# Attention in a four-layer transformer stack: values as the stationary operand with a block of ones for the sums, and a new order at the opening and at the seam

## What is computed

```python
for l in range(4):
    h = rmsnorm(x, n1[l])
    q, k, v = split(h @ Wqkv[l].T + bqkv[l])                 # 16 heads of 8
    o = merge_heads(softmax(rope(q) @ rope(k).T * 8 ** -0.5 + causal) @ v)
    x = x + o @ Wo[l].T + bo[l]
    h2 = rmsnorm(x, n2[l])
    kc, vc = split(memory @ Wkv_c[l].T)
    x = x + merge_heads(softmax((h2 @ Wq_c[l].T) @ kc.T * 8 ** -0.5 + cross_bias) @ vc) @ Wo_c[l].T
    h3 = rmsnorm(x, n3[l])
    x = x + silu(h3 @ Wg[l].T) * (h3 @ Wu[l].T) @ Wd[l].T
```

## Time and profile before

| | |
|---|---|
| median of 3 runs | 500.36 us (498.70 to 501.63) |
| the profiled execution: own time, span | 499.64 us, 497.5 us |
| PE busy, PEld busy | 465.2 us (94%), 401.7 us (81%) |
| DVE, ACT, POOL busy | 358.0 us (72%), 268.5 us (54%), 227.9 us (46%) |
| opening until the first projection (L608) | 0 to 16.8 us |
| four layers | to 214.9 us |
| seam until the next block runs steadily | 214.9 to some 226 us |
| later blocks | to 497.5 us |

### The profile page before, as it was taken

How to read it: one execution, slowest core, us unless ns; L and a number is a source line. 1 busy time by engine, 2 the same in 40 slices (tenths; PEclk the granted TensorE clock), 3 DMA queues, 4 the chain that set the end, 5 groups by cost and what they waited for, 6 DMA issues and landing times. The chain is left out here.

```text
span 497.5 us, 14297 instructions
## 1 busy us (share of the span) xinstructions
PE 465.2 (94%) x5430; PEld 401.7 (81%) x5430; DVE 358.0 (72%) x1025; ACT 268.5 (54%) x718; POOL 227.9 (46%) x342
## 2 busy tenths in 40 slices
PE   3899999999999999968999998899999998999997
PEld 3667887788778876967999887789999887689997
DVE  4395668566856786656887889999989987654643
ACT  4377757775777577614334475556466554442221
POOL 2871377137613851243799322767889322300000
PEclk9999999999999999979999999999999999999999
DMA  8601020101029000040210432031020000000000
GB/s 252 276 3 32 10 84 2 40 22 65 3 64 381 2 3 1 2 130 17 70 49 24 157 111 67 2 133 60 10 69 3 2 1 1 1 2 1 12 1 12
DMA packets 9953, 27.08 MB, mean 54 GB/s; under 512 B 1346, under 2 KB 4759, under 8 KB 9623
## 3 DMA queue, kind: packets, MB, share of 16 engines
q1 hardware_dynamic: 9878, 26.09, 15.5%
HBM read 25.82 MB, written 0.26 MB: 52 GB/s over the span
## 5 line engine op out<-in xcount | busy, mean ns | idle before, releaser
L913 POOL TENSOR_TENSOR rstd<-ss,par 128x1 f32<-128x1 f32 x52 | 28.5, 549 | 100.8 <-ACT sq L737 100.8
L759 ACT ACTIVATE pr<-sd 128x512 f32<-128x512 f32 x56 | 34.5, 626 | 5.4 <-DVE sd L816 4.9
L1243 POOL TENSOR_TENSOR xh<-xh,rsx 128x512 f32<-128x512 f32 (+1 forms) x32 | 29.8, 931 | 2.5
L1241 POOL TENSOR_TENSOR xh<-cx,mvx 128x512 f32<-128x512 f32 (+1 forms) x32 | 29.4, 918 | 2.7 <-DMA cx<-ctx_in 1.4
L741 ACT ACTIVATE h<-y,rstd 128x128 f32<-128x128 f32 x48 | 19.1, 399 | 9.5 <-POOL rstd L913 9.4
L1222 DVE BATCH_NORM_STATS2 stx<-cx 128x6 f32<-128x128 f32 x104 | 22.7, 276 | 0.5 <-DMA cx<-ctx_in 0.5
L1772 POOL TENSOR_TENSOR rstd<-mv,par 128x1 f32<-128x1 f32 x20 | 4.1, 207 | 39.8 <-DVE mv L1602 36.3
L737 ACT ACTIVATE sq<-y 128x129 f32<-128x129 f32 x52 | 15.9, 306 | 10.0 <-DVE y L847 8.6
L907 POOL TENSOR_TENSOR kblk<-qk,cf 128x512 f32<-128x512 f32 x20 | 20.8, 1040 | 0.9
L1232 POOL TENSOR_TENSOR rsx<-rsx,par 128x13 f32<-128x13 f32 x8 | 20.4, 2546 | 0.6
L1791 POOL TENSOR_SCALAR rk<-kss 128x8 f32<-128x8 f32 (+1 forms) x32 | 7.5, 235 | 24.0 <-DVE kss L1668 22.5
(11 more groups left out here) (570 smaller groups left out, 1507.2 us busy)
## 6 DMA issues: line engine op xcount, KB each, us to landing
cx<-ctx_in SPq DMA_DIRECT2D x13, 768.0 KB
we<-we_in SPq DMA_DIRECT2D x8, 514.0 KB, 7.1
wc<-wc_in SPq DMA_DIRECT2D x4, 768.5 KB, 5.8
wa<-wa_in SPq DMA_DIRECT2D x5, 387.0 KB, 3.0
wb<-wb_in SPq DMA_DIRECT2D x4, 256.5 KB, 3.8
uvT<-uvT_in SPq DMA_DIRECT2D x1, 1024.0 KB, 7.1
uv<-uv_in SPq DMA_DIRECT2D x1, 1024.0 KB, 8.6
cx<-ctx_in SPq DMA_DIRECT2D x13, 32.5 KB
```

The source lines that it names most:

```text
L759: nc.scalar.activation(pr[:, t, at:at + 512], sd[:, t, at:at + 512], ACT.Exp).then_inc(s[piece], 1)
L913: nc.gpsimd.tensor_tensor(rstd[:, t:t + 1], ss[:, t:t + 1], par[:, 1:2], ALU.pow).then_inc(s[piece], 1)
L1241: step(pool, "pool_step", nc.gpsimd.tensor_tensor(part, cx[u % 2][:, tiles, :], mvx[:, b, tiles, 0].unsqueeze(2).to_broadcast(shape), ALU. ...
L1243: nc.gpsimd.tensor_tensor(part, part, rsx[:, b, tiles].unsqueeze(2).to_broadcast(shape), ALU.mult).then_inc(xm["c_normed"], 1)
```

## The change

1. In `weigha`, `weighb` and `cweigh` the operands change places. The values, spread with zeros to 32 columns (vblk and vcblk), are the stationary operand, and 64 tokens of the turned weights are moving. Four products with 32 columns each write the four groups of 32 rows of one bank. Four more products per half (`ones8` stationary, 128 tokens moving) write the sums next to them, each repeated in 8 rows. A half is 8 + 4 products instead of 8.
2. The result comes out turned. turn_o, oT, cturn_o and coT are gone; `recip` and `crecip` now take 128 x 128 instead of 128 x 16, and `o` and `co` write oT. The bias of the values moves into vblk, whose two copies become two additions (L806 before).
3. `out` reads the rows of Wo in another order (`heads`), made on the host.
4. The opening: x is the first transfer, seg_in comes as one row first and spread later; `mem4` is copied by DVE instead of ACT; vblk and vcblk are cleared by one POOL memset, and by no other piece; memory, mem_k, kc and mem_v of layer 0 go in between the pieces of its self-attention (`FIRST`).
5. The seam: on PE `fast` is now the Else, so that PE jumps over `whole` at the start. ACT's four square_f and what DVE does after z_norm of tile 1 stand behind the If. All tables have new numbers, and so the queues a new order.

```diff
             elif piece in ("weigha", "weighb"):
-                for j in range(4 * (half == "b"), 4 * (half == "b") + 4):
-                    for b in range(2):
-                        last = nc.tensor.matmul(bank[L * b:L * b + L, 18 * j:18 * j + 18], pts[:, t, P * j + L * b:P * j + L * b + L],
-                                                vblk[:, t, b, j, :, :], start=True, stop=True)
+                for b in range(2):
+                    for k in range(4):
+                        j = 4 * half + k
+                        at = 32 * j - 16 * half
+                        nc.tensor.matmul(bank[32 * k:32 * k + 32, L * b:L * b + L], vblk[:, t, b, at:at + 32],
+                                         pts[:, t, P * j + L * b:P * j + L * b + L], start=not half and b == 0, stop=True, skip_group_check=True)
+                for k in range(4):
+                    j = 4 * half + k
+                    last = nc.tensor.matmul(bank[32 * k:32 * k + 32, P:2 * P], ones8[:, 16 - 16 * half:48 - 16 * half], pts[:, t, P * j:P * j + P],
+                                            start=False, stop=True, skip_group_check=True)
                 last.then_inc(s[piece], 1)
-            elif piece in ("turn_o", "cturn_o"):
+            elif piece == "cturn_o":
...
-                pe.wait_ge(s["oT"], n)
+                pe.wait_ge(s["o"], n)
...
-            elif piece == "oT":
-                act.wait_ge(s["turn_o"], n)
-                nc.scalar.activation(oT[:, t, :], held(od, "turn_o", l, t)[:, 0:P], ACT.Identity,
-                                     bias=A[:, A_BV:A_BV + 1]).then_inc(s["oT"], 1)
...
-                nc.vector.reciprocal(rv[:, t, :], ops[:, :, 8]).then_inc(s[piece], 1)
+                nc.vector.reciprocal(qk[:, t, 0, :], held(od, k, l, t)[:, P:2 * P]).then_inc(s[piece], 1)
...
-                nc.vector.tensor_tensor(o[:, t, :].rearrange("p (h d) -> p h d", d=HD), ops[:, :, 0:8],
-                                        rv[:, t, :].unsqueeze(2).to_broadcast([P, H, HD]), ALU.mult).then_inc(s[piece], 1)
+                nc.vector.tensor_tensor(oT[:, t, :], held(od, k, l, t)[:, 0:P], qk[:, t, 0, :], ALU.mult).then_inc(s[piece], 1)
...
         def sp_opening(sp):
-            sp.dma_start(segr[:], seg_in.to_broadcast([P, B * L])).then_inc(s["seg_loaded"], 16)
             sp.dma_start(x[:], x_in.rearrange("(t p) d -> p t d", p=P)).then_inc(s["x_loaded"], 16)
+            sp.dma_start(segi[:], seg_in).then_inc(s["row_loaded"], 16)
+            sp.dma_start(cf[:], cf_in).then_inc(s["cf_loaded"], 16)
+            load_a(sp, 0)
             sp.dma_start(memT[:], memT_in).then_inc(s["mem_loaded"], 16)
             load_b(sp, 0)
...
-                either(pe, lambda: opening(pe, x_pe_piece, pe_piece, "PE"), whole)
+                either(pe, lambda: opening(pe, x_pe_piece, pe_piece, "PE"), whole, falls="end")
```

More of the change, by code:

```diff
@@ L55 @@
 CG = [range(c, min(c + 4, CT)) for c in range(0, CT, 4)]
-PERIOD, SKEW = 95.43, (0.0, 6.74, 13.36, 19.85)
+PERIOD, SKEW = 95.50, (0.0, 6.67, 13.27, 19.91)
 AT = {
[L62 to L74, removed]
@@ new lines @@
+    "PE": {"memory": -54.70, "turn1": -6.09, "project": 0.00, "values": 3.82, "causal": 13.16, "scores": 13.61,
+           "turna": 21.31, "turnb": 21.52, "weigha": 22.05, "weighb": 25.05, "out": 30.41, "turn2": 36.31, "qc": 38.94,
+           "cmask": 41.20, "cscores": 41.43, "cturn": 49.89, "cweigh": 53.17, "cturn_o": -343.21, "cout": 56.79,
+           "turn3": 63.35, "gate": 68.43, "up": 70.12, "down": 81.04},
+    "ACT": {"square1": -15.22, "norm1": -9.46, "mem_k": -47.81, "hT1": -6.71, "q_groups": 8.81, "expa": 15.57,
+            "expb": 18.42, "turneda": 19.96, "turnedb": 21.09, "square2": 29.73, "norm2": 33.72, "hT2": 34.50,
+            "qcT": 36.40, "cexp": 45.30, "cturned": 47.91, "coT": -343.21, "square3": 58.24, "norm3": 59.91,
+            "hT3": 64.58, "tanh": 66.74},
@@ L79 @@
 HOLDS = {
-    1: {"memory": ("mem_k", "mem_v"), "turn1": ("hT1",), "turna": ("turneda",), "turnb": ("turnedb",), "weigha": ("o",), "turn_o": ("oT",), "out": ("y1",), "turn2": ("hT2",),
+    1: {"memory": ("mem_k", "mem_v"), "turn1": ("hT1",), "turna": ("turneda",), "turnb": ("turnedb",), "weigha": ("o",), "out": ("y1",), "turn2": ("hT2",),
         "qc": ("qcT",), "cturn": ("cturned",), "cweigh": ("co",), "cturn_o": ("coT",), "cout": ("y2",), "turn3": ("hT3",),
@@ L86 @@
 BEHIND = "cturn_o cout turn3 gate up down coT square3 hT3 tanh y2 norm3 gated hidden y3 pow3".split()
-SELF = ("turn1 project values causal scores turna turnb weigha weighb turn_o out hT1 q_groups expa expb turneda turnedb oT rope vblk "
+SELF = ("turn1 project values causal scores turna turnb weigha weighb out hT1 q_groups expa expb turneda turnedb rope vblk "
         "maxa maxb shifta shiftb recip o y1 "
@@ L122 @@
 LAYER = {e: list(pieces) for e, pieces in AT.items()}
-FINAL = {"PE": {}, "ACT": {"square_f": 0.18}, "DVE": {"norm_f": 4.73, "x_f": 6.55, "z_moments": 10.88, "z_norm": 17.41},
-         "POOL": {"pow_f": -7.85, "z_power": 0.96}}
+FINAL = {"PE": {}, "ACT": {"square_f": 44411.67}, "DVE": {"norm_f": 37724.60, "x_f": 37726.01, "z_moments": 37727.40, "z_norm": 37735.68},
+         "POOL": {"pow_f": 35574.92, "z_power": 41054.99}}
 for e in AT:
     PLACE.update({p: PLACE["y3"] - PERIOD + a for p, a in FINAL[e].items()})
-FAST = Order({e: [(p, range(LAYERS)) for p in LAYER[e]] + [(p, [LAYERS]) for p in FINAL[e]] for e in AT}, late)
+TURNED = ("cturn_o", "coT")
+FAST = Order({e: [(p, range(LAYERS)) for p in LAYER[e] if p not in TURNED] + [(p, [LAYERS]) for p in FINAL[e]] for e in AT}, late)
 GENERAL = Order({e: [(p, range(LAYERS)) for p in LAYER[e] if p not in CROSS] + [(p, [LAYERS]) for p in FINAL[e]]
@@ L245, in __init__ @@
                       for e in AT}
-        self.first = {e: 1 + max(n for n, z in enumerate(q) if z[1] == 0) for e, q in self.queue.items()}
+        self.first = {e: 1 + max(n for n, z in enumerate(q) if z[1] == 0 and not (e == "ACT" and z[2] == LAYERS) and
+                                 not (e == "DVE" and z[2] == LAYERS and z[3:] != (1, "z_norm"))) for e, q in self.queue.items()}
+        self.rest = {z[2:] for e, q in self.queue.items() for z in q[self.first[e]:] if z[1] == 0}
         FAST.bank, LAST.bank = {}, {}
```

231 lines of the change are left out of this document (127 added, 104 removed).

## The result

The changed kernel takes 502.64 us (median of 20 runs), the kernel before 499.25 us (20 runs): a ratio of 1.0062, with an interval of 1.0045 to 1.0080. It is 0.6% slower where no change was forecast. The profiled execution took 501.80 us against 499.64, its span 500.0 against 497.5, so that the traces hold 2.5 of the roughly 3 us.

The account below looks back on a forecast made before the run. The prediction took PE's queue to bound the kernel in the layers. Its terms, −2.3 − 0.7 − 3.1 + 1.1 + 2.0 + 1.2 + 1.4 + 0.5, summed to +0.1, so 499.7 us, with a range of 493 to 508.

Parts of the forecast that it names:

- Reciprocal: On DVE in the layers: 1.0 us for 128x128, 0.74 more each, delaying PE by +1.4 us in four layers.
- weigh: On PE: 56 halves at 0.50 us instead of 0.48, +1.1 us in all.
- The turns: On PE: 36 turns of o removed at 0.11 us each, less 0.9 for waits that grow, −3.1 us.
- the new wait: In the layers: weigha waits for ACT's copy behind adjacent turna and turnb of tile 0, once per layer, +1.2 us.
- modes: On PE in the four layers: 12 more changes of array part size at 0.17 us each, +2.0 us.
- The opening: Start of the kernel: first scores 3.0 us earlier despite PE's jump, one memory of 0.67 still to do, −2.3 us.
- The later blocks: In the last attention: longer chains from weighb through recip to out, +0.5 us.
- Rival B: In the layers: DVE makes PE wait, maxima standing behind long reciprocals; 506.3 or 507.7 us, chance 0.16.
- A: Layers and start: charged waits and mode changes fall into PE's free time, start gives −3.5; 493.4 us, chance 0.32.
- C: On PE: pitch of starts doesn't fall, 0.72 us a half instead of 0.48; 512.0 us, chance 0.09.
- D: On PE: only two column groups work at once, 1.0 us a half; 527.7 us, chance 0.03.
- seam: Between layers and later blocks: down starts some 0.7 us earlier, z_turn some 2.9 us after y3 of tile 3; −0.7 us.

Follow-up runs that it names:

- experiments 3: Changed kernel with the layer numbers of before (PERIOD, SKEW, AT), without turn_o and oT, two opening numbers later; 1.0243 of the kernel before.
- 5: Changed kernel with the numbers of before in layers 1 to 3 on all engines; 0.9972 of the kernel before.
- experiment 15: Changed kernel with PE's numbers of before in layers 1 to 3 and PE's jump back at the seam, run again; 0.9981 of the kernel before, median 499.39 us.
- Experiment 8: Changed kernel with PE's If as before, so that PE jumps at the seam; 1.0044 of the kernel before.
- experiment 2: Kernel before with the reciprocal working on 128 columns, nothing else moved; 1.0300 of the kernel before.
- 7: Kernel before without turn_o, oT, cturn_o and coT; 0.9882 of the kernel before.
- 10: Changed kernel with PE's numbers of before in layers 1 to 3 and PE's jump back at the seam; 0.9940 of the kernel before.
- 11: Changed kernel with all engines' numbers of before in layers 1 to 3 and PE's jump back at the seam; 0.9954 of the kernel before.
- 13: Kernel before without turn_o, oT, cturn_o and coT and with the reciprocal over 128 columns; 0.9922 of the kernel before.
- experiment 1: Changed kernel with its reciprocals working on 16 of the 128 columns; 1.0013 of the kernel before.

## Why the forecast was wrong

**The terms of the change itself were near.** Reciprocal: 1.0 us forecast, 0.95 measured; DVE 39.7 a layer forecast, 39.05 measured. weigh: +0.02 a half forecast, 0.00 measured. z_turn was forecast at 2.9 us behind y3: it is 2.8. The turns: −3.1 forecast; alone they are −1.07 a layer, −4.3 in four, made of 1.51 less work and 0.44 more idle time a layer. So a turn takes more than the 0.11 of its step, and the waits that grow are 1.8 in four layers instead of 0.9. The reciprocal was forecast at +0.35 a layer; it is 0.65 in the order of the changed kernel and 1.0 in that of before.

**The step that failed is the one for the new order of the rows**, "the new wait" and "modes". I charged +1.2 for one wait a layer and +2.0 for 12 more mode changes, 0.8 a layer. Read against experiments 3, 5 and 15, in which the same operations in the order of before take 48.6 to 48.9, the new order costs 50.45 − 48.9 = 1.5 a layer, twice that. I had looked at one place, where turna and turnb of tile 0 stand together and weigha was to wait. There is no wait there: the turns end at 129.75 and weigha starts at 129.80. PE waits 0.33 ahead of these turns, 0.33 at the weigh at 134.11, where the earlier trace rows had 0.22, and most of all in the cross-attention, which the forecast did not look at: 2.3 us in two layers ahead of cweigh and cout, against 0.4 before and none in experiment 15. Waits are only a part of it. Of the 1.52 us between the periods of the changed kernel and of experiment 15 (50.45 and 48.93), 0.68 is idle time of PE and 0.84 is time in which it works. Whether that is the mode changes, which I had at 0.5 a layer, no run shows. The last layer, without memory pieces, costs 0.25 more than before, the layers with them 1.7; that points at the place of these pieces, but no run moved them alone, nor any other piece of PE's row.

**The opening was mis-sized**, −2.3 for −0.6. The jump takes 5.57 us there, not 3.84; project starts at 14.11, not at 12.9 to 13.8, and I took the first scores at 20.5, where this and a wait of 0.64 for POOL make it 21.8. Experiment 8 shows what PE's If is worth: 3.6 us at project, 1.9 at the first down.

**The later blocks were not looked at.** I charged +0.5. They are 1.9 shorter in the one trace, the size of one stop behind the seam, which is in the trace of before and, with 1.35, in that of experiment 2, but not in 7, 8, 10, 11, 13 and 15, which jump at the seam too. Where the stop is absent in the order of before, the jump is longer (4.87 and 4.98 us in 7 and 13, 3.84 and 3.50 in before and 2). One thing goes with it in the traces: in the two with the stop SP issues the first of the next block's transfers (xw) as z_turn starts, at 217.29 and 217.45, and at 229.63 and 229.51 in 2; in 8, 10, 11 and 15 it does so 5.0 us behind z_turn, in 7 and 13 1.3 and 1.4 ahead of it. No run moved these transfers alone, so what makes the stop is open.

**Rival B** (DVE) had the right place and the wrong victim: not the maxima but turn_o waits for o, and only in the order of before with its turns (experiment 2, +15 us; I had said up to +8). Since the change takes these turns away together with making the reciprocal longer, B did not come. A, C and D did not either. Two numbers of the forecast do not follow from its own terms: its +2.6 for the layers is a period of 49.4, not 48.5 to 48.9, and B with 0.3 for each of 32 reciprocals and the last attention fully paid is 499.7 + 9.6 − 1.4 + 2.5 = 510.4, not 507.7.

In all, +0.1 was forecast, made of −2.3, +2.6 for the layers, −0.7 and +0.5; the trace has −0.6, +5.3, −0.3 and −1.9. That the sum is off by only 2.4 us is partly luck: opening, layers and seam were 4.8 too low, and the later blocks, for no reason that I had given, 2.4 too high.

## What to carry to other kernels

The price of a longer instruction is set by who stands right behind it on the engine that is the bound. Eight reciprocals a layer, each 0.7 us longer, were worth 3.4 us with a consumer placed just where the result had been ready, and 1.0 without it; so look for the consumer whose place in the queue has no slack, before looking at the engine's busy share. A change that comes with a new order is two changes: run the new operations in the old order first. Here the operations alone are free or a small gain (0.2% and 0.6% under before, with PE's old order in layers 1 to 3 and its old If), and the new order of PE's row takes it back.

## What the runs showed of the hardware

- The taken branch on PE lasts 3.4 to 5.0 us at the seam (eight traces) and 5.2 to 6.5 us in the opening (nine traces), with 3.84 and 5.57 in the kernels before and after. Where it falls through it takes 0.09. In experiment 8 it cost nothing at the seam, since another chain was as long.
- In the idle time at the seam the granted clock falls to 0.50, the lower of the two levels, and stays there for some 7 us in the traces of before, after and experiment 8 (from 216, 221 and 220 us on), with or without a jump. The execution of experiment 1 had a mean of 0.91 and 0.89 in two stretches of the later blocks, and kept almost nothing of what it had gained; whether the one made the other was not tried.
- Executions of one kernel differ with their mean granted clock. In run 15 five with 0.993 took 497.0 to 498.2 us and four with 0.983 took 501.7 to 502.3; in run 10 seven with 0.993 took 495.9 to 497.7 and two with 0.983 took 501.7 and 502.2. The changed kernel had 0.993 or more in 11 of 12 executions beside run 15. So how often the clock is lower is a part of each median: at 0.993 alone run 15 has a mean of 497.7 against 502.8 for the changed kernel, which is 1.0% and within what I had expected.
- On parts of 128x32, PE's weight loads followed each other at 17 ns (16 in 0.27 us), and a half of weigh with 64 and 128 moving columns took the 0.58 us that one with 18 moving columns took on parts of 128x64.
